# A sort by permutation matmuls, moved in part to indirect DMA writes, and a gather ring of 16 rows

## Chip, cores, metric

The kernel runs on one core of one Trainium2 chip. The metric is the device time of one execution in microseconds. Engines are named as in the profile: PE (TensorE), DVE (VectorE), ACT (ScalarE), POOL (GpSimd), SP (SyncE). POOL can issue DMAs whose row addresses stand in SBUF (indirect DMAs).

## The reference, cut to what matters

Four layers on x of 1250 x 1024 with 21250 edges (src, dst, type 0 to 7, weight), sorted by dst. Only the first two speak of edges:

```python
h  = sigmoid(layernorm(x) @ wenc.T + benc)            # 1250 x 500
h2 = h @ conv_weight
agg = segment_sum(h2[src] * edge_weight[:, None], dst)
x = x + ((agg + h @ lin_weight.T) @ wdec.T + bdec)    # layer 0, graph part
# dense mixture of 4 experts; then layer 1, graph part:
for r in range(8):                                    # relations
    out += (segment_sum(x[src] * (type == r), dst) / max(count[r], 1)) @ weight[r]
# gate, then 8 routed experts
```

## The kernel before

**Slots.** Rows are padded to 1280, ten tiles of 128. The edges come in as a 128 x 167 table (ET = 167 columns; partition p holds edges 167p to 167p + 166). They are regrouped into 176 slots (SLOTS) of 128 lanes, so that all edges of a slot go to one tile of destination rows. DVE computes for each edge its place, a lane and a slot (`sort`, lines 1213 to 1242, and lines 1281 to 1285), and packs source, relation and row into one number (`e_pack`, lines 1286 to 1288).

**The list.** To move each edge to its place, PE multiplies: for each of the 167 columns DVE builds a 128 x 128 matrix of lanes (`perm_lane`, line 1296) and a 128 x 352 matrix that holds pack and weight in the column of the slot (`perm_val`, lines 1297 and 1298), in a ring of four, and PE accumulates `perm_lane.T @ perm_val` in one PSUM bank (`permute`, line 622). PE has 120 of these put between other matmuls by `next_column` (line 629): one behind each matmul of the encoder from its third group on (80, line 643) and behind each of the h2 product (40, line 661). The other 47 run in a loop of PE behind them (lines 668 to 674). Then follow on PE the ten tiles of `h @ lin` (`from_h(A_LIN, KE)`, line 677, its matmuls also line 661), which ACT copies into `agg`. Meanwhile DVE unpacks the list out of PSUM (lines 1312 to 1322) and signals `list_ready`.

**Slot sums of layer 0.** For each slot POOL gathers 128 rows of h2 (2 KB each) from DRAM by an indirect DMA (`gather_slots`, line 521) into a ring of 8 rows (RING) in the region `room`. It runs in a loop: a copy of eight indices into `at_ring` (line 512) once in eight slots, and a wait for PE once in four (BATCH). ACT makes the weighted one-hot matrix of the slot, from one that DVE made for four slots at once (lines 1339 and 1340). PE multiplies both with the gathered rows (`slot_sum`, line 680: matmuls of lines 685 and 686) into one of four PSUM banks. DVE loads the slot's tile number into a register (line 1346) and adds the bank to that tile of `agg` (line 1351), each add behind the one before. PE may be four slots ahead of DVE, POOL eight ahead of PE. The wait of POOL for the first ring row that is used again lies behind PE's lin products, as slot sums do.

**Afterwards.** The decoder reads `agg` by transposes; then come the experts of layer 0, the relation products and root and gate products of layer 1 (PE, in split precision), in whose time POOL gathers 176 x 128 inverse counts of 4 bytes (line 540), then the slot sums of layer 1 (line 521 again, rows of 4 KB, PE lines 820 and 821, DVE line 1535), the gate, and the routed experts. The kernel ends with ten unrolled indirect gathers of POOL (line 575), each followed by an add of DVE (line 1701) and a store.

**Queues.** SP issues the plain loads in program order: edges, x, weights, constants; then waits for the encoder to load the decoder weights and the decoder bias, and for the slot sums before the experts' weights.

Of the kernel before, what the change touches and what calls it, by code (L numbers as in the profile page):

```python
# [30 lines left out]
P = 128  # L31
# [13 lines left out]
RING = 8  # L45
BATCH = 4
SLOTS = -(-((N_EDGES + NT * (P - 1)) // P) // RING) * RING
# [4 lines left out]
E1 = 8  # L52
# [4 lines left out]
NOWHERE = 1.0e6  # L57
# [5 lines left out]

UNIT_ENC, UNIT_CONVLIN, UNIT_DEC = 0, 1, 2
# [42 lines left out]
def build(nc, a, out):  # L107
    ctx = ExitStack()
    with ctx:
# [16 lines left out]
        moe_dram = dram("moe_rows", (TSLOTS * P, D))  # L126

# [18 lines left out]
        rows_h2 = room[:].rearrange("p b (c n) -> p (b c) n", n=EMBP)  # L146
# [46 lines left out]
        e_slot = scratch(ET)  # L193
        e_pack = e_key
# [112 lines left out]
        (rows_in,) = sems(RING, "rows_in")  # L307
# [55 lines left out]
        def _(sp):  # L363
# [39 lines left out]
            sp.wait_ge(slot_summed, RING + SLOTS)  # L403
# [42 lines left out]
            sp.wait_ge(slot_summed, RING + 2 * SLOTS)  # L446
# [40 lines left out]
        def _(pool):  # L487
# [17 lines left out]

            def gather_slots(table, at_list, rows, done, rounds_done):

                with pool.Fori(0, SLOTS // (2 * RING)) as i:
                    for half in range(2):


                        pool.tensor_copy(at_ring[:, half, :], at_list[:, bass.ds(2 * RING * i + half * RING, RING)]).then_inc(at_ready, 1)  # L512
                        for k in range(RING):
                            if k % BATCH == 0:

                                pool.wait_ge(slot_summed, done + 2 * RING * i + half * RING + k + BATCH)
# [11 lines left out]
            gather_slots(h2_dram, l_src, lambda k: rows_h2[:, k, :], 0, 0)  # L528
# [4 lines left out]
            pool.wait_ge(rows_in[RING - 1], 16 * SLOTS // RING)  # L533
            inv_rows = inv_dram.rearrange("n (r o) -> (n r) o", o=1)
            with pool.Fori(0, SLOTS // RING) as i:
                pool.tensor_copy(at_ring[:, 0, :], l_inv_at[:, bass.ds(RING * i, RING)]).then_inc(at_ready, 1)
                pool.wait_ge(at_ready, SLOTS // RING + i + 1)
# [15 lines left out]
            gather_slots(y_dram.rearrange("n r d -> (n r) d"), l_row8, lambda k: rows_y[:, k, :], SLOTS, 2 * SLOTS // RING)  # L553
# [4 lines left out]
            rounds = 3 * SLOTS // RING  # L558
# [22 lines left out]
        def _(pe):  # L581

            mm = nc.tensor.matmul
            pe.sem_inc(slot_summed, RING)
# [95 lines left out]
            def slot_sum(i, k, first=False):  # L680
                if not first or k >= 4:
                    pe.wait_ge(slot_added, RING * i + (k - 3))
                pe.wait_ge(hot_ready, RING * i + k + 1)
                pe.wait_ge(rows_in[k], 16 * i + 16)
                mm(sum_bank[k % 4][:, EMBC:EMBP], hot1[:, k, :], hotr[:, k, :], start=True, stop=True)
                mm(sum_bank[k % 4][:, 0:EMBC], hot[:, k, :], rows_h2[:, k, 0:EMBC], start=True, stop=True).then_inc(slot_summed, 1)  # L686
# [126 lines left out]
            def slot_sum2(i, k, first=False):  # L813
# [4 lines left out]
                pe.wait_ge(rows_in[k], 16 * i + 16 * (SLOTS // RING) + 16)  # L818
# [107 lines left out]
        def _(act):  # L926
# [34 lines left out]
            for m in range(NT):  # L961
                q = A_LIN + m
                act.wait_ge(a_full, q + 1)
                if m == 0:
                    act.wait_ge(perm_done, ET)
# [199 lines left out]
        def _(dve):  # L1165
# [47 lines left out]
            def sort(key, groups, cols, onehot, cum, pos, bank, full, tmp, between=lambda: None):  # L1213
# [25 lines left out]
                v.tensor_scalar(tmp, key, float(groups), NOWHERE, ALU.is_ge, ALU.mult)  # L1239
# [28 lines left out]
            link(v.tensor_copy(e_key, e_t0))  # L1268

# [8 lines left out]
            sort(e_key, NT, ET, e_hot, e_cum, e_pos, v_bank[0], V_PRE, e_lane, first_ln)  # L1278
# [10 lines left out]
            dve.wait_ge(room_zero, 1)  # L1289
# [12 lines left out]
            tail = (ET - head) % 4  # L1302
            for t in range(head):
                permute(t, t % 4, first=True)
            with dve.Fori(0, (ET - head - tail) // 4) as i:
                for j in range(4):
                    permute(4 * i + head + j, j)
            for t in range(ET - tail, ET):
# [33 lines left out]
            def add_slots(i, b, first=False):  # L1342

                for k in range(BATCH * b, BATCH * (b + 1)):
# [3 lines left out]
                    dve.wait_ge(slot_summed, RING * i + (RING + k + 1))  # L1348
# [182 lines left out]
            def add_slot2(i, k, first=False):  # L1531
                t = dve.value_load(l_tile[0:1, k:k + 1] if first else l_tile[0:1, bass.ds(RING * i + k, 1)], min_val=0, max_val=NT - 1)
                dve.wait_ge(slot_summed, RING * i + (SLOTS + RING + k + 1))
# [68 lines left out]
            sort(tok_key[:], E1, NT, tok_hot[:], tok_cum[:], tok_pos[:], v_bank[V_PRE2 % 2], V_PRE2, gsm[:, 0, :])  # L1602
# [131 lines left out]
```

## Time and profile before

| | us |
|---|---|
| median of three executions | 3163.37 |
| lowest, highest of them | 3155.08, 3163.69 |
| span of the profiled execution | 3157.0 |
| PE busy in it | 2859.9 (91%) |
| DVE, ACT, POOL busy in it | 1363.6, 592.5, 564.0 |
| mean clock granted to PE | 0.950 |

The span runs from the first instruction to the last of one more execution, taken by the profiler; its own time outside the span is not among the numbers shown, so the span is set beside the median. A matmul with float32 operands stands in the trace as two records. "Idle before" is the time that an engine stood still ahead of an instruction, with what ended it; "issue" means nothing that the profile shows. A clock of 1.00 is 2.4 GHz, 0.50 is 1.2 GHz.

### The profile page before, as it was taken

Reading aid. Unit: us, or ns where it says so; the run is one execution under the profiler, and the core shown is the slowest. Engines: PE = TensorE matmul, PEld = TensorE weight load, DVE = VectorE, ACT = ScalarE, POOL = GpSimd, SP = SyncE. Lnnn points to the kernel's source line nnn. Section 1 sums busy time; section 2 is a strip of 40 time slices with the busy share of each in tenths; the row PEclk is TensorE's granted clock in tenths of the full one; section 3 lists DMA queues with packets and bytes.
Section 4 is the critical chain, followed back from the end, with each engine's and each line's share of the span. In section 5 each row is a group of like instructions: output and inputs, shape, how many; then the busy total and the mean of one; then the engine's idle time right before and its main releaser. Section 6 shows DMA issues by size and latency. Waiting matters only on the chain.

```text
span 3157.0 us, 36610 instructions
## 1 busy us (share of the span) xinstructions
PE 2859.9 (91%) x11166; PEld 2026.2 (64%) x11166; DVE 1363.6 (43%) x2560; ACT 592.5 (19%) x1089; POOL 564.0 (18%) x673
## 2 busy tenths in 40 slices
PE   6999777879999997999999999999989998958884
PEld 3653222338888776888888888888854445836663
DVE  7664555454555464101001010112158887845453
ACT  2001121122333322212112121211010001123330
POOL 0002566100000002555400000000035551000001
PEclk9999888979999997999999999999999999979997
DMA  3012555203332323222212222311268883236664
GB/s 124 0 67 68 160 156 161 67 1 107 121 111 97 124 80 114 80 98 73 103 73 103 73 103 73 116 57 33 95 224 304 301 308 133 80 150 216 223 223 176
DMA packets 165619, 392.69 MB, mean 124 GB/s; under 512 B 22158, under 2 KB 22670, under 8 KB 165560
## 3 DMA queue, kind: packets, MB, share of 16 engines
q1 hardware_dynamic: 81208, 174.26, 15.8%
q0 software_dynamic: 49072, 153.09, 15.2%
q10 hardware_dynamic: 35280, 64.54, 5.5%
q8 instruction: 38, 0.62, 0.1%
q14 instruction: 21, 0.17, 0.0%
HBM read 316.94 MB, written 74.89 MB: 124 GB/s over the span
## 4 chain that ended last, share of the span: by engine, by line
PE 71%; DVE 7%; issue 4%; DMA 3%; DVEq 2%; ACT 2%; POOL 1%; ACTq 0%; SPq 0%; POOLq 0%; another core or an unknown queue 0%
PE pair L796 12%; PE pair L798 12%; PE pair L797 12%; PE pair L820 5%; PE pair L821 5%; PE pair L686 3%; PE pair L707 2%; PE pair L762 2%; PE pair L744 2%; PE pair L764 2%; PE pair L763 2%; PE pair L746 2%; PE pair L745 2%; DVE wl L1433 2%; DMA tok_raw<-in_L_ffn_w 2%
## 5 line engine op out<-in xcount | busy, mean ns | idle before, releaser
L796 PE MATMUL pair<-wh,xh 128*128 128x512 f32 x1600 | 623.4, 390 | 1.8 <-DVE xl L1185 1.8
L798 PE MATMUL pair<-wl,xh 128*128 128x512 f32 x1600 | 623.1, 389 | 0.0
L797 PE MATMUL pair<-wh,xl 128*128 128x512 f32 x1600 | 623.1, 389 | 0.0
L1433 DVE TENSOR_TENSOR wl<-raw,wh 128x512 fp32r<-128x512 f32 x352 | 221.5, 686 | 804.0 <-ACT wh L929 755.2
L796 PEld LDWEIGHTS pair<-wh,xh 128*128 128x128 f32 x1600 | 300.8, 188 | 64.6 <-issue 2.2
L797 PEld LDWEIGHTS pair<-wh,xl 128*128 128x128 f32 x1600 | 300.8, 188 | 62.7
L798 PEld LDWEIGHTS pair<-wl,xh 128*128 128x128 f32 x1600 | 300.7, 188 | 62.5
L929 ACT ACTIVATE wh<-raw 128x512 fp32r<-128x512 f32 x352 | 208.0, 627 | 334.8 <-PE pair L764 164.0
L929 ACT ACTIVATE OS<-pair 128x512 f32<-128x512 f32 x170 | 101.3, 596 | 742.7 <-PE pair L798 618.6
L1535 DVE TENSOR_TENSOR X<-pair,X 128x1024 f32 x176 | 215.5, 1225 | 52.5 <-PE pair L821 37.8
L686 PE MATMUL pair<-room,XN 128*128 128x504 f32 x352 | 215.2, 728 | 0.0
L1351 DVE TENSOR_TENSOR U<-pair,U 128x512 f32 x176 | 121.7, 691 | 167.1 <-PE pair L686 63.3
L521 POOL DMA_INDIRECT room<-h_rows,at_ring x176 | 169.1, 961 | 133.9 <-PE pair L686 69.2
L820 PE MATMUL pair<-W,XN 128*128 128x512 f32 x352 | 181.3, 597 | 9.4 <-DMA W<-y_rows,at_ring 9.1
L521 POOL DMA_INDIRECT W<-y_rows,at_ring x176 | 165.4, 940 | 136.1 <-PE pair L821 92.6
L540 POOL DMA_INDIRECT inv_ring<-inv_count,at_ring x176 | 169.2, 961 | 67.9 <-issue 50.4
L821 PE MATMUL pair<-W,XN 128*128 128x512 f32 x352 | 180.6, 595 | 0.0
L744 PE MATMUL pair<-xh,wh 128*128 128x384 f32 (+1 forms) x384 | 138.5, 361 | 10.1 <-DVE wl L1433 10.1
L512 POOL COPY at_ring<-l_row 128x8 int32 x22 | 4.4, 200 | 760.9 <-PE pair L798 760.8
L762 PE MATMUL pair<-wh,hh 128*128 128x512 f32 x320 | 126.6, 396 | 12.9 <-DVE hl L1469 11.2
L745 PE MATMUL pair<-xl,wh 128*128 128x384 f32 (+1 forms) x384 | 137.5, 358 | 0.0
L746 PE MATMUL pair<-xh,wl 128*128 128x384 f32 (+1 forms) x384 | 137.4, 358 | 0.0
(249 smaller groups left out, 3732.7 us busy)
## 6 DMA issues: line engine op xcount, KB each, us to landing
y_rows<-OS ACTq DMA_DIRECT2D x160, 256.0 KB
raw<-in_L_gnn_weight SPq DMA_DIRECT2D x16, 2048.0 KB
raw<-in_L_ffn_w SPq DMA_DIRECT2D x12, 2048.0 KB
raw<-in_L_ffn_w SPq DMA_DIRECT2D x24, 1024.0 KB
tok_raw<-in_L_ffn_w SPq DMA_DIRECT2D x7, 2048.0 KB
tok_raw<-in_L_ffn_w SPq DMA_DIRECT2D x14, 1024.0 KB
U<-in_L_ffn_b SPq DMA_DIRECT2D x18, 512.0 KB
moe_rows<-OS ACTq DMA_DIRECT2D x36, 256.0 KB
```

What stands on the lines that cost most here:

```text
L521: pool.indirect_dma_start(rows(k), None, table, bass.IndirectOffsetOnAxis(ap=at_ring[:, half, k:k + 1], axis=0)).then_inc(rows_in[k], 16)
L686: mm(sum_bank[k % 4][:, 0:EMBC], hot[:, k, :], rows_h2[:, k, 0:EMBC], start=True, stop=True).then_inc(slot_summed, 1)
L744: mm(o, wh[:, k, part], xh[:, k, cols], start=(k == 0), stop=False)
L745: mm(o, wh[:, k, part], xl[:, k, cols], start=False, stop=False)
L796: mm(o, xh[:, k, cols], wh[:, k, :], start=(k == 0), stop=False)
L797: mm(o, xl[:, k, cols], wh[:, k, :], start=False, stop=False)
L798: last = mm(o, xh[:, k, cols], wl[:, k, :], start=False, stop=(k == KD - 1))
L820: mm(pair[:, 0:HALF], hot[:, k, :], rows_y[:, k, 0:HALF], start=True, stop=True)
L821: mm(pair[:, HALF:D], hot[:, k, :], rows_y[:, k, HALF:D], start=True, stop=True).then_inc(slot_summed, 1)
L929: return nc.scalar.activation(dst, src, func, **kw)
L1433: v.tensor_tensor(wl[:, k, :], raw[:, k, :], wh[:, k, :].bitcast(F32), ALU.subtract).then_inc(wl_ready, 1)
L1535: v.tensor_tensor(u_rows[:, bass.ds(t, 1), :], pairs[(k + 1) % 4][:].rearrange("p (o n) -> p o n", o=1), u_rows[:, bass.ds(t, 1), :], ALU. ...
```

## The change

120 of the 167 columns (SCATTERED) are no longer permuted. The place of an edge is turned into the number of a row of 8 bytes (pack and weight) in a DRAM table `list_dram`, lane times 176 plus slot. SP fills the table with zeros early, DVE makes indices and records (`e_at`, `e_rec`, in the second half of XN), and POOL writes each of the 120 columns with an indirect DMA, 128 records at a time. When all have landed SP loads the table back (`l_part`), and DVE adds it to what PE has accumulated of the other 47 columns. Padding edges get places beyond the part that is read (NOWHERE). PE's 47 permutes all stand between encoder matmuls; the loop behind h2 is gone.

The gathers of layer 0 are unrolled, take their indices from the list itself, and use a ring of 16 rows (RING0) in the region XT, which is free then. All counts that start with the ring's size are shifted. One wait of POOL ahead of the inverse counts, for the last gathered row, is gone.

```diff
+RING0 = 16
+SCATTERED = 120
-NOWHERE = 1.0e6
+NOWHERE = float((1 << 20) + P - 1)
+PERMUTED = ET - SCATTERED
+        list_rows = (P - 1) * SLOTS + (int(NOWHERE) >> 7) + ET
+        list_dram = dram("list_rows", (list_rows + 1, 2))
-        rows_h2 = room[:].rearrange("p b (c n) -> p (b c) n", n=EMBP)
+        rows_h2 = XT[:].rearrange("p k n -> p (k n)")[:, 0:RING0 * EMBP].rearrange("p (b n) -> p b n", n=EMBP)
+        e_rec = XN[:, 1, 0:2 * ET].rearrange("p (t c) -> p t c", c=2)
+        e_at = XN[:, 1, 2 * ET:3 * ET].bitcast(I32)
+        l_part = XN[:, 1, 3 * ET:3 * ET + 2 * SLOTS].rearrange("p (s c) -> p s c", c=2)
...
+            sp.wait_ge(room_zero, 1)
+            sp.dma_start(list_dram[0:P * SLOTS, :].rearrange("(p s) c -> p (s c)", s=SLOTS), room[:, 0, 0:2 * SLOTS]).then_inc(list_zero, 16)
+            sp.wait_ge(scattered, 16 * SCATTERED)
+            sp.dma_start(l_part, list_dram[0:P * SLOTS, :].rearrange("(p s) c -> p s c", s=SLOTS)).then_inc(list_in, 16)
             sp.wait_ge(a_full, A_H2)
             dec = W[:, UNIT_DEC % 2, :].rearrange("p (k n) -> p k n", k=KE)
             sp.dma_start(dec, wide(a["decT"])).then_inc(w_in[UNIT_DEC % 2], 16)
...
-            sp.wait_ge(slot_summed, RING + SLOTS)
+            sp.wait_ge(slot_summed, RING0 + SLOTS)
...
+            pool.wait_ge(list_zero, 16)
+            pool.wait_ge(scatter_ready, 1)
+            for t in range(ET - SCATTERED, ET):
+                pool.indirect_dma_start(list_dram, bass.IndirectOffsetOnAxis(ap=e_at[:, t:t + 1], axis=0),
+                                        e_rec[:, t, :], None).then_inc(scattered, 16)
...
-            gather_slots(h2_dram, l_src, lambda k: rows_h2[:, k, :], 0, 0)
+            for s in range(SLOTS):
+                if s >= RING0 and s % BATCH == 0:
+                    pool.wait_ge(slot_summed, s + BATCH)
+                pool.indirect_dma_start(rows_h2[:, s % RING0, :], None, h2_dram,
+                                        bass.IndirectOffsetOnAxis(ap=l_src[:, s:s + 1], axis=0)
+                                        ).then_inc(rows_in[s % RING0], 16)
...
-            pool.wait_ge(rows_in[RING - 1], 16 * SLOTS // RING)
...
-            pe.sem_inc(slot_summed, RING)
+            pe.sem_inc(slot_summed, RING0)
...
-            column = iter(range(ET))
+            column = iter(range(PERMUTED))
...
             def next_column():
-                t = next(column)
-                permute(t, t % 4, first=(t == 0))
+                t = next(column, None)
+                if t is not None:
+                    permute(t, t % 4, first=(t == 0), final=(t == PERMUTED - 1))
...
             from_h(A_H2, 0, next_column)
-            begun = next(column)
-            tail = (ET - begun) % 4 or 4
-            with pe.Fori(0, (ET - begun - tail) // 4) as i:
-                for j in range(4):
-                    permute(4 * i + begun + j, (begun + j) % 4)
-            for t in range(ET - tail, ET):
-                permute(t, t % 4, final=(t == ET - 1))
...
-            for k in range(RING):
+            for k in range(RING0):
                 slot_sum(0, k, first=True)
-            with pe.Fori(1, SLOTS // RING) as i:
-                for k in range(RING):
+            with pe.Fori(1, SLOTS // RING0) as i:
+                for k in range(RING0):
                     slot_sum(i, k)
...
-                v.tensor_scalar(tmp, key, float(groups), NOWHERE, ALU.is_ge, ALU.mult)
+                v.scalar_tensor_tensor(tmp, key, float(groups), far, ALU.is_ge, ALU.mult)
...
+            v.tensor_scalar(e_slot, iota_free[:, 0:ET], float(P), NOWHERE, ALU.mult, ALU.add)
...
-            dve.wait_ge(room_zero, 1)
+            dve.wait_ge(t_full, T_LN1 + 2 * NT)
+            v.tensor_copy(e_rec[:, :, 0], e_pack)
+            v.tensor_copy(e_rec[:, :, 1], e_w)
+            link(v.scalar_tensor_tensor(e_at, e_lane, float(SLOTS), e_slot, ALU.mult, ALU.add))
+            v.sem_inc(scatter_ready, 1)
+            dve.wait_ge(list_zero, 16)
...
-            dve.wait_ge(perm_done, ET)
-            v.tensor_copy(l_w[:], list_bank[:, SLOTS:2 * SLOTS])
-            link(v.tensor_copy(l_pack[:], list_bank[:, 0:SLOTS]))
+            dve.wait_ge(perm_done, PERMUTED)
+            dve.wait_ge(list_in, 16)
+            v.tensor_tensor(l_w[:], list_bank[:, SLOTS:2 * SLOTS], l_part[:, :, 1], ALU.add)
+            link(v.tensor_tensor(l_pack[:], list_bank[:, 0:SLOTS], l_part[:, :, 0], ALU.add))
```

## Rows read from the trace of the kernel before

**Rows 1.** The page: the chain that ended last, by engine
```profile
PE 71%; DVE 7%; issue 4%; DMA 3%; DVEq 2%; ACT 2%; POOL 1%; ACTq 0%; SPq 0%; POOLq 0%; another core or an unknown queue 0%
```

**Rows 2.** Windows, by stage: us, busy us (instructions) of PE, PEld, DVE, ACT, POOL; clock; DMA
```profile
57.35:217.67 160.32, 160.30 (x480) 90.81 (x479) 103.84 (x369) 12.07 (x20) 0.00 (x0) 1.00 0.08 28
217.67:252.88 35.21, 35.21 (x98) 14.81 (x96) 33.86 (x134) 0.60 (x1) 0.00 (x0) 1.00 0.07 23
...
288.35:577.97 289.62, 217.79 (x529) 73.81 (x529) 150.91 (x260) 55.65 (x175) 166.94 (x188) 0.85 0.55 152
```

**Rows 3.** Timeline, interleaved stretch: start, us, engine, line, tiles [idle before]
```profile
208.11 1.02 PE L661 MATMUL pair<-W,U 128*128 128x512 f32 x2
...
209.56 1.02 PE L661 MATMUL pair<-W,U 128*128 128x512 f32 x2
```

**Rows 4.** Timeline, from the last permute to the first gather
```profile
252.88 34.50 PE L661 MATMUL pair<-W,U 128*128 128x512 f32 x80
...
256.08 0.34 DVE L1322 SCALAR_TENSOR_TENSOR l_inv_at<-l_tmp,l_rel 128x176 int32<-128x176 f32 x1
...
258.34 1.17 POOL L521 DMA_INDIRECT room<-h_rows,at_ring  x1 [0.92 <-POOL at_ring L512]
```

**Rows 5.** Timeline, the ninth gather; source L521, who waited for it
```profile
293.30 0.97 POOL L521 DMA_INDIRECT room<-h_rows,at_ring  x1 [24.83 <-PE pair L686]
...
  PEld pair L685: 22.0, 12
  PE pair L685: 13.7, 22
```

**Rows 6.** Timeline, DVE ahead of the permutes
```profile
56.33 0.33 DVE L1286 SCALAR_TENSOR_TENSOR U<-U 128x167 f32<-128x167 int32 x1
...
57.35 0.29 DVE L1296 TENSOR_SCALAR room<-iota_free,U 128x128 f32<-128x128 f32 x1
```

**Rows 7.** Timeline of POOL, end of a round of count gathers
```profile
1241.80 0.94 POOL L540 DMA_INDIRECT inv_ring<-inv_count,at_ring  x1 [0.30 <-issue]
1244.78 0.19 POOL L545 COPY l_inv<-inv_ring 128x8 f32 x1 [2.04 <-DMA inv_ring<-inv_count,at_ring]
```

**Rows 8.** Timeline, first and last of the ten unrolled gathers at the end
```profile
3126.13 0.94 POOL L575 DMA_INDIRECT XT<-moe_rows,tok_posi  x1 [53.91 <-DMA moe_rows<-OS]
...
3140.23 1.81 POOL L575 DMA_INDIRECT XT<-moe_rows,tok_posi  x1 [0.30 <-issue]
```

**Rows 9.** DMA issues of the whole span: xcount, KB, us to landing
```profile
W<-in_decT SPq DMA_DIRECT2D x1, 2048.0 KB, 7.7
...
b_dec<-in_L_gnn_bdec SPq DMA_DIRECT2D x1, 512.0 KB, 3.6
...
inv_count<-count ACTq DMA_DIRECT2D x1, 40.0 KB, 7.5
```

**Rows 10.** Timeline, a held add and PE's wait for it
```profile
355.37 0.69 DVE L1351 TENSOR_TENSOR U<-pair,U 128x512 f32 x1 [3.55 <-remote]
...
356.30 0.17 PE L685 MATMUL pair<-hotr,hot 128*128 128x8 bf16 x1 [3.12 <-DVE U L1351]
```

**Rows 11.** Waits, slot stage of layer 0: us, times, longest
```profile
POOL room L521 <- PE pair L686: 69.2, 17, 24.8
```

**Rows 12.** Windows of L1351 (adds), then L521 (gathers): us, busy (x), clock, DMA
```profile
399.00:412.00 13.00, 8.09 (x12) 0.75 0.47 126
424.00:438.00 14.00, 4.15 (x6) 0.76 0.62 180
508.00:524.00 16.00, 4.45 (x7) 0.93 0.69 192
...
399.00:412.00 13.00, 7.43 (x8) 0.75 0.47 126
424.00:438.00 14.00, 8.10 (x8) 0.76 0.62 180
508.00:524.00 16.00, 9.85 (x12) 0.93 0.69 192
```

More of the change, by code:

```diff
@@ L306, in build @@
         (os_out,) = sems(4, "os_out")
-        (rows_in,) = sems(RING, "rows_in")
+        (rows_in,) = sems(RING0, "rows_in")
+        list_zero, scatter_ready, scattered, list_in = map(sem, ("list_zero", "scatter_ready", "scattered", "list_in"))
         (moe_in,) = sems(NT, "moe_in")
@@ L444, in _ @@
                 sp.dma_start(raw1[j][:], wide(top[1][4 * j * P:4 * (j + 1) * P, :])).then_inc(raw1_in, 16)
-            sp.wait_ge(slot_summed, RING + 2 * SLOTS)
+            sp.wait_ge(slot_summed, RING0 + 2 * SLOTS)
             for k in range(4):
@@ L514, in gather_slots @@
                             if k % BATCH == 0:
-                                pool.wait_ge(slot_summed, done + 2 * RING * i + half * RING + k + BATCH)
+                                pool.wait_ge(slot_summed, done + 2 * RING * i + half * RING + k + BATCH + RING0 - RING)
                                 pool.sem_inc(issued, 1)
@@ L667, in _ @@
             from_h(A_H2, 0, next_column)
-            begun = next(column)
-            tail = (ET - begun) % 4 or 4
-            with pe.Fori(0, (ET - begun - tail) // 4) as i:
-                for j in range(4):
-                    permute(4 * i + begun + j, (begun + j) % 4)
-            for t in range(ET - tail, ET):
-                permute(t, t % 4, final=(t == ET - 1))
+            assert next(column, None) is None
             from_h(A_LIN, KE)
@@ L681, in slot_sum @@
                 if not first or k >= 4:
-                    pe.wait_ge(slot_added, RING * i + (k - 3))
-                pe.wait_ge(hot_ready, RING * i + k + 1)
+                    pe.wait_ge(slot_added, RING0 * i + (k - 3))
+                pe.wait_ge(hot_ready, RING0 * i + k + 1)
                 pe.wait_ge(rows_in[k], 16 * i + 16)
-                mm(sum_bank[k % 4][:, EMBC:EMBP], hot1[:, k, :], hotr[:, k, :], start=True, stop=True)
-                mm(sum_bank[k % 4][:, 0:EMBC], hot[:, k, :], rows_h2[:, k, 0:EMBC], start=True, stop=True).then_inc(slot_summed, 1)
-            for k in range(RING):
+                mm(sum_bank[k % 4][:, EMBC:EMBP], hot1[:, k % RING, :], hotr[:, k % RING, :], start=True, stop=True)
+                mm(sum_bank[k % 4][:, 0:EMBC], hot[:, k % RING, :], rows_h2[:, k, 0:EMBC], start=True, stop=True).then_inc(slot_summed, 1)
+            for k in range(RING0):
                 slot_sum(0, k, first=True)
-            with pe.Fori(1, SLOTS // RING) as i:
-                for k in range(RING):
+            with pe.Fori(1, SLOTS // RING0) as i:
+                for k in range(RING0):
                     slot_sum(i, k)
@@ L964, in _ @@
                 if m == 0:
-                    act.wait_ge(perm_done, ET)
+                    act.wait_ge(perm_done, PERMUTED)
                 copy(agg[:, m, :], a_bank[q % 2][:]).then_inc(a_read, 1)
@@ L1211, in keep_scores, with sort @@
                     v.tensor_copy(rows[0:n, lo:lo + cnt], v_bank[(q + g) % 2][0:n, 0:cnt]).then_inc(v_read, 1)
-            def sort(key, groups, cols, onehot, cum, pos, bank, full, tmp, between=lambda: None):
+            def sort(key, groups, cols, onehot, cum, pos, bank, full, tmp, far, between=lambda: None):
                 gs = slice(0, groups)
@@ L1276, in first_ln @@
                 normalise(1, T_LN1)
-            sort(e_key, NT, ET, e_hot, e_cum, e_pos, v_bank[0], V_PRE, e_lane, first_ln)
+            sort(e_key, NT, ET, e_hot, e_cum, e_pos, v_bank[0], V_PRE, e_lane, e_slot, first_ln)
             slot_groups(l_tile[:], l_tmp[:], SLOTS, NT)
@@ L1301, in _ @@
             head = 4
-            tail = (ET - head) % 4
+            tail = (PERMUTED - head) % 4
             for t in range(head):
                 permute(t, t % 4, first=True)
-            with dve.Fori(0, (ET - head - tail) // 4) as i:
+            with dve.Fori(0, (PERMUTED - head - tail) // 4) as i:
                 for j in range(4):
                     permute(4 * i + head + j, j)
-            for t in range(ET - tail, ET):
+            for t in range(PERMUTED - tail, PERMUTED):
                 permute(t, t % 4)
-            dve.wait_ge(perm_done, ET)
-            v.tensor_copy(l_w[:], list_bank[:, SLOTS:2 * SLOTS])
-            link(v.tensor_copy(l_pack[:], list_bank[:, 0:SLOTS]))
+            dve.wait_ge(perm_done, PERMUTED)
+            dve.wait_ge(list_in, 16)
+            v.tensor_tensor(l_w[:], list_bank[:, SLOTS:2 * SLOTS], l_part[:, :, 1], ALU.add)
+            link(v.tensor_tensor(l_pack[:], list_bank[:, 0:SLOTS], l_part[:, :, 0], ALU.add))
             link(v.tensor_scalar(l_row8[:], l_pack[:], (1 << ROWSHIFT) - 1, None, ALU.bitwise_and))
@@ L1601, in _ @@
             link(v.tensor_tensor(tok_key[:], top_f[:, :, 0], tok_pad[:], ALU.add))
-            sort(tok_key[:], E1, NT, tok_hot[:], tok_cum[:], tok_pos[:], v_bank[V_PRE2 % 2], V_PRE2, gsm[:, 0, :])
+            v.tensor_scalar(gsm[:, 1, :], iota_free[:, 0:NT], 0.0, NOWHERE, ALU.mult, ALU.add)
+            sort(tok_key[:], E1, NT, tok_hot[:], tok_cum[:], tok_pos[:], v_bank[V_PRE2 % 2], V_PRE2, gsm[:, 0, :], gsm[:, 1, :])
             slot_groups(slot_exp[:], slot_tmp[:], TSLOTS, E1)
```

12 lines of the change are left out of this document (6 added, 6 removed).

## The prediction

> **What bounds the kernel now.** I read the page's chain first [rows 1]: PE holds 71% of it, so a microsecond taken from work beside PE is worth nothing unless PE waits there, or does work that the change removes. The table by stage [rows 2] shows such places. After 577.97 us nothing that the change touches costs time. Before it lie four stretches: the encoder and h2 matmuls with 120 permutes between them (57.35 to 217.67, PE full), the 47 permutes left over (217.67 to 252.88, PE full), the lin matmuls (to 288.35), and the slot sums (to 577.97), where PE is busy 217.79 of 289.62 us, its granted clock is 0.85, and no engine is full.
>
> In the first stretch [rows 3] one 128x512 matmul, a permute and the next matmul take 1.45 us (208.11 to 209.56). The 40 lin matmuls of that size (two records each) take 34.50 us, 0.86 each [rows 4], so a permute between matmuls costs PE 0.59 us. The 47 left over go at 35.21/47 = 0.75 us, the pace of the three DVE instructions that make their operands. Then comes the hand-over [rows 4]: the last permute ends at 252.88, DVE has unpacked the list at 256.42, the first gather goes at 258.34. Eight gathers lie ready early; the ninth waits for a ring row until 293.30, because PE does lin first [rows 5].
>
> **Part 1, the sort.** PE loses 73 interleaved permutes, 73 x 0.59 = 43 us, and the stretch of the 47, 35 us. It would be through with lin at 288 - 43 - 35 + 1 = 211 us. But the list now needs 120 DMA writes first, and they set its time:
> - DVE starts permuting at 57.35, and the write indices are made just before that: two copies and one scalar_tensor_tensor on 128x167, which go at 0.34 us each there (three from 56.33 to 57.35 [rows 6]), and two small additions in and before the sort, 0.3 together: 1.3 us. Ready at 58.6; POOL wakes 0.3 us after a DVE signal, as I count from 256.42: 58.9. The indices' wait for the layer norm's transposes costs nothing, PE being in the encoder by 57.35 [rows 2].
> - POOL issues an indirect DMA each 1.25 us (0.94 busy, 0.30 between), for 4-byte pieces as for rows of 2 KB [rows 5, 7]. No row prices a write by index. From below: 1.25 us, for the same 128 descriptors. From above: the unrolled gathers at the end, nine steps in 3140.23 - 3126.13 = 14.1 us, 1.57 each [rows 8], which run beside VectorE adds. I take 1.25, as nearest in kind are the small pieces. With 0.2 for a slower first one and 119 x 1.25 the last goes at 207.9 and lands 2.98 us later (1241.80 to 1244.78 [rows 7]), 210.9.
> - The DMA engines' own part: the count store is 1280 pieces of 32 B, 80 for each of 16 engines, and lands in 7.5 us [rows 9], at most 0.09 us a piece. A column has 8 per engine, 0.75 us, under the 1.25 of the issue, so POOL hides it; the price if it does not is a rival below.
> - SP fetches the 180 KB back. A load of 512 KB landed in 3.6 us [rows 9]; I take 2.8 and 0.3 to wake: 214.0. The decoder weights, queued on SP behind that wait, leave some 48 us later. They are used at 580, so being late costs nothing, but their 2 MB take 7.7 us [rows 9] and meet the first gathers: 2 us.
> - DVE's unpacking stays 3.4 us, POOL wakes in 0.3: first gather at 217.7 instead of 258.34. PE idles from 211, so the list, not PE, sets the start.
>
> The first row lands about 3.1 us on, so slot sums start at 220.8 instead of 288.35: 67.5 us earlier. Against that stand 2 us because PE begins after ten idle microseconds, at the low clock (stretches with a restart show 0.75 [rows 12]), and the 2 us of the decoder weights.
>
> **Part 2, the ring of 16 and the unrolling.** They remove POOL's waits for PE in this stage, 69.2 us in 17 waits, of which the first, 24.8, is already counted above [rows 11], and POOL's copy and second wait once in eight. What this could reach is POOL's own pace, 176 x 1.25 = 220 us in place of 289.6, a gain of 69. But PE waited for gathered rows only 22.0 + 13.7 = 35.7 us [rows 5]. What holds the stage is DVE's add: that of 355.37 came after 3.55 idle us, with the sum long there, and PE then stood 3.12 us for it, four banks being all it has [rows 10]. Between two adds DVE only loads the tile number into a register (line 1346). In stretches the adds come slow or quick [rows 12]: in 399 to 412 there are 12, one per 1.08 us, with 8 gathers; in 424 to 438 and 508 to 524 there are 13 in 30 us with 20 gathers, while POOL goes on without a stop.
> - So POOL's lead falls by 4/13 = 0.31 a us in the quick stretch and grows by 7/30 = 0.23 in the slow ones. Where the two balance, 43% of the time is quick and a slot takes 1/(0.43 x 12/13 + 0.57 x 13/30) = 1.55 us, near the measured 289.6/176 = 1.65. The ring's size is not in this sum: it makes the swings longer and leaves their mix. I take no gain and no loss. The loss side: quick stretches half as common, 1/(0.215 x 0.92 + 0.785 x 0.43) = 1.86 us a slot, +38 us. The gain side: -69.
> - The rest ends at nothing: the second slot stage only gets shifted counts, and the wait of POOL that goes ahead of the inverse counts lies far before PE's first relation product, for which POOL waits anyway. The later layers move as they are.
>
> **Sum.** -67.5 + 2 + 2 = -63.5 us against the profiled execution: 3157.0 - 63.5 = 3093.5 of span. The median shown, 3163.37, is 6.4 above that span, so I forecast 3100 us. A measurement of this kernel can tell 0.3%, 9.5 us, from nothing.
>
> **The rivals.**
> - *The ring pays (0.18).* If DVE's held loads come with POOL's stops and restarts, or if the deeper lead keeps PE at full clock, the stage goes at the 1.25 us of the issue: 3100 - 69 = 3031. For it: the clock is 0.75 and 0.76 in two of the three stretches [rows 12], and slots at low clock are slower than POOL. Against it: the slow adds lie within POOL's long runs, and a deeper ring makes these longer.
> - *The writes go slower beside VectorE, or the slow stretches grow (0.17).* At the 1.57 us of the unrolled gathers [rows 8] the list is 120 x 0.32 = 38 us later: 3138, with PE idle 48 us ahead of the slot sums. The loss side of part 2 gives 3138 too. For it: DVE is busy 103.84 of 160.32 us beside the interleaved permutes [rows 2], here until the 47 are done, at 126. Against it: that covers 54 of the 120 writes. The Trainium skill, "SBUF — State Buffer", section "Who interferes with whom", says that copy and tensor_scalar can enter a mode that holds the port pair shared with GpSimd for a whole instruction. By that rule each of the 54 could be held for one instruction of DVE of some 0.3 us [rows 6], 16 us in all: 3116.
> - *Slower: the small writes themselves take the time (0.08).* The place is the DMA engines from 59 us to the list. If a column's writes had to be finished before the next one's began, a column would cost the 2.98 us of a landing [rows 7] in place of 1.25: 120 x 1.73 = 208 us later, 3308. It decides from 1.25 + 63.5/120 = 1.78 us a column; above that the list comes too late for any gain. Against it: the count gathers come each 1.25 us without waiting for each other's landings, and the store of small pieces landed in 7.5 us [rows 7, 9]. The Trainium skill, "DMA: Bandwidth & Descriptors", section "Specifications", says that a transfer under 512 B does a read-modify-write; no row here has writes of 8 B.
> - *The forecast as worked out (0.57),* 3085 to 3115.
>
> **Range and chances.** Forecast and first two rivals hold 0.92. The range 3028 to 3145 takes them in and leaves out the slow tail. Faster by over 0.3% (under 3154): 0.57 + 0.18 + most of 0.17, which can come with other small losses: 0.87. Within 0.3%: 0.05. Slower: 0.08.
>
> **What would show it.** Right: 120 DMA issues of POOL from about 59 us at 1.25; 47 permutes, all before 127; PE through with lin near 211 and idle to 221; slot sums over 280 to 295 us, with adds still in quick and slow stretches; all after them moved by one amount. Wrong: a pitch of the writes over 1.3 us, or their last landing over 5 us; a slot stage under 270 or over 305 us, or adds that are held differently; a first gather far behind the last write, which would put a cost on SP's queue.

## The result, and the profile after

The changed kernel took 3203.43 us (median of four, 3196.76 to 3210.92) against 3160.04 for the kernel before on the same chip: ratio 1.0143, interval 1.0122 to 1.0164. It is 43 us slower where 60 faster was forecast. The profiled execution took 3201.72 us at a span of 3199.9. Later runs show that this sign goes with the chip: on another chip the same kernel is 2.8% faster. So each time below stands against the kernel before on the same chip.

First GpSimd's writes and SP's fetch of the list, by tile (first and last start):

```profile
L522 POOL DMA_INDIRECT list_rows<-XN x120: 954/958/1271, 58.9 to 212.2; - x120
L406 SPq DMA_DIRECT2D XN<-list_rows x1: 320/320/320, 214.3 to 214.3; - x1
```

These are the steps of the forecast, the last write 4 us after its 207.9. But the table of windows, with the columns of [rows 2], over the time of the writes and over the slot sums reads:

```profile
57.00:218.00 161.00, 62.20 (x108) 24.98 (x106) 24.95 (x82) 2.06 (x3) 115.35 (x120) 0.63 0.02 2
...
343.00:623.60 280.60, 209.75 (x529) 78.82 (x529) 150.29 (x260) 55.78 (x176) 157.10 (x160) 0.82 0.54 150
```

PE is busy 62 of 161 us where it was full [rows 2], and the clock falls to 0.63. The timeline of DVE shows a column each 11.2 us in place of 1.45 ("remote" names a releaser that the profile can't place), until three columns start 0.8 us apart once POOL has been silent for 15 us:

```profile
156.82 0.29 DVE L1320 TENSOR_SCALAR room<-iota_free,U 128x128 f32<-128x128 f32 x1 [10.32 <-remote]
...
200.93 0.29 DVE L1320 TENSOR_SCALAR room<-iota_free,U 128x128 f32<-128x128 f32 x1 [10.30 <-remote]
212.12 0.35 DVE L1320 TENSOR_SCALAR room<-iota_free,U 128x128 f32<-128x128 f32 x1 [10.13 <-remote]
221.94 0.29 DVE L1320 TENSOR_SCALAR room<-iota_free,U 128x128 f32<-128x128 f32 x1 [8.71 <-remote]
227.57 0.28 DVE L1320 TENSOR_SCALAR room<-iota_free,U 128x128 f32<-128x128 f32 x1 [4.79 <-remote]
228.39 0.28 DVE L1320 TENSOR_SCALAR room<-iota_free,U 128x128 f32<-128x128 f32 x1
229.16 0.28 DVE L1320 TENSOR_SCALAR room<-iota_free,U 128x128 f32<-128x128 f32 x1
```

PE, in its timeline, takes each column about 1 us after DVE began it:

```profile
157.85 1.54 PE L645 MATMUL pair<-room 128*128 128x352 f32 x2 [8.04 <-DVE room L1322]
```

DVE may not make a column before PE has read the one four back. An engine learns that another is done by a counter that the other raises; I call that a signal. The column of 200.93 needed the signal of the one that DVE began at 156.82 and PE multiplied at 157.85 to about 159.4. So DVE learned some 42 us late of a matmul that had ended. The other direction is prompt. ScalarE learns late too. Here are its next two evictions after that of 69.42, and ahead of the second the matmul of PE that it needed, the last of its group of eight:

```profile
140.58 0.69 ACT L969 ACTIVATE U<-pair,b_enc 128x512 f32<-128x512 f32 x1 [70.47 <-remote]
180.76 1.83 PE L667 MATMUL pair<-XT,W 128*128 128x512 f32 x2
227.41 0.69 ACT L969 ACTIVATE U<-pair,b_enc 128x512 f32<-128x512 f32 x1 [86.14 <-remote]
```

About half of the 86.14 us is PE's own slow group, which needs eight columns. But that matmul had ended at 182.6, so 45 us of the wait are the signal's. It was sent between those of the permutes at 179.43 and 190.68, and it came at 227.41, between the columns of 221.94 and 227.57 that these two released. PE's signals thus arrive in the order in which they were sent, though they go to two engines.

The rest follows. The encoder and h2 are late, and the first row gather waits for the last store of h2 (timeline of POOL):

```profile
212.21 0.96 POOL L522 DMA_INDIRECT list_rows<-XN  x1 [0.30 <-issue]
312.42 1.00 POOL L550 DMA_INDIRECT XT<-h_rows,l_src  x1 [99.25 <-DMA h_rows<-OS]
```

Slot sums run from 343.1 to 623.6 in place of 288.35 to 577.97 [rows 2]: they begin 55 us later and take 9 us less. After them the kernel is the same.

### The profile page after: what moved, and what is told of

The parts are those of the page before. It is cut to its first block, busy times and chain, and to the rows that moved or that the text cites. A ratio compares the mean times of both kernels' runs of the same rounds, so it can differ in the third digit from the quotient of the medians.

```text
span 3199.9 us, 35021 instructions
## 1 busy us (share of the span) xinstructions
PE 2796.1 (87%) x10926; PEld 1991.2 (62%) x10926; DVE 1267.8 (40%) x2205; ACT 591.9 (18%) x1089; POOL 674.1 (21%) x771
## 4 chain that ended last, share of the span: by engine, by line
PE 74%; DVE 9%; another core or an unknown queue 4%; issue 4%; DMA 3%; DVEq 3%; ACT 2%; POOL 0%; ACTq 0%; SPq 0%; POOLq 0%
PE pair L814 11%; PE pair L816 11%; PE pair L815 11%; PE pair L838 5%; PE pair L839 5%; PE pair L704 3%; PE pair L725 2%; PE pair L685 2%; PE pair L762 2%; PE pair L764 2%; PE pair L763 2%; PE pair L780 2%; PE pair L782 2%; PE pair L781 2%
## 5 line engine op out<-in xcount | busy, mean ns | idle before, releaser
L550 POOL DMA_INDIRECT XT<-h_rows,l_src x176 | 172.3, 979 | 224.1 <-DMA h_rows<-OS 99.2
L704 PE MATMUL pair<-XT,XN 128*128 128x504 f32 x352 | 208.7, 733 | 0.0
L645 PE MATMUL pair<-room 128*128 128x352 f32 x94 | 46.2, 579 | 106.0 <-issue 73.2
```

The source lines that it names most:

```text
L550: pool.indirect_dma_start(rows_h2[:, s % RING0, :], None, h2_dram, bass.IndirectOffsetOnAxis(ap=l_src[:, s:s + 1], axis=0)).then_inc(rows_ ...
L704: mm(sum_bank[k % 4][:, 0:EMBC], hot[:, k % RING, :], rows_h2[:, k, 0:EMBC], start=True, stop=True).then_inc(slot_summed, 1)
```

## The experiments

The runs fell on two kinds of chip. On some, the one of the first result among them, the kernel before took 3153 to 3160 us; I call these the **late** chips. On two others it took 3114 and 3117 us, the **prompt** chips. One late chip was met twice and was late both times; no other is known to have been, so whether this is the chip itself or a state that lasts is not shown. The expectations stand as written before each run; those of the first four kernels (e1 to e4) know nothing yet of two kinds.

**Ring and unrolling alone** (late: 3154.23 against 3155.82; prompt: 3080.61 against 3114.19).

```diff
-SCATTERED = 120
+SCATTERED = 0
...
```

The rest of the edit takes out the writes and the fetch of the list and puts PE's loop of 47 permutes back.

> Only the ring of 16 and the unrolled gathers; no edge column is written by GpSimd, all 167 are permuted. Theory (a long unbroken stream of indirect DMAs from GpSimd makes the other engines learn of TensorE's signals tens of microseconds late): the sort is as in the kernel before, permutes at 1.45 us a column, lin done near 288 us, because GpSimd is silent there; the slot sums have the gathers beside them as before and take 280 to 290 us; time 3150 to 3165. Rival (the unrolled gathers or the ring of 16 are what costs the 43 us): 3200. Rival from the prediction (the ring pays): slot sums near 220 us, time 3090.

> Ring of 16 and unrolled gathers alone, once more, for a chip on which the signals are late (kernel before 3158 us). There the slot sums should take about 280 us as in the changed kernel, in place of 290 us (rows ready ahead: 16 in place of 8), begin near 288 us and the time be 3145 to 3158. If it were the ring or the unrolling that costs, 3200. On a chip that takes 3114 us for the kernel before: 3081 us again.

Ratios 0.9892 (0.9876 to 0.9909) on a prompt chip and 0.9989 (0.9973 to 1.0005) on a late one. So these parts don't cost the 43 us. And the same instructions give two slot stages: 288.7 to about 503 us on the prompt chip, 288.6 to 580 on the late one. The adds of DVE show why; here by tile, what they waited for and who waited for them, first prompt, then late:

```profile
L1367 DVE TENSOR_TENSOR U<-pair,U x176: 682/691/693, 290.0 to 502.7; 128x512 f32 x176
...
  PE pair L701: 77.8, 88
  DVE U L1367: 14.5, 48
  issue: 1.4, 9
...
  PEld pair L700: 9.2, 14
```

```profile
  issue: 88.0, 58
  PE pair L701: 46.1, 19
...
  remote: 13.8, 3
...
  PE pair L700: 53.7, 26
```

On the late chip the adds stand 102 us for "issue" and "remote", and PE's matmuls stand 53.7 us for adds; on the prompt one the adds stand 1.4 us so, and only weight loads stand for them, 9.2 us. That is the held add of [rows 10].

**DVE's permutes written out**, waits and addresses constant (prompt: 3028.89 against 3114.19; late: 3200.93 against 3158.05).

```diff
-            with dve.Fori(0, (PERMUTED - head - tail) // 4) as i:
-                for j in range(4):
-                    permute(4 * i + head + j, j)
-            for t in range(PERMUTED - tail, PERMUTED):
+            for t in range(head, PERMUTED):
```

> The changed kernel with VectorE's loop of permutes written out, so that its waits compare with constants and its addresses are constants. Theory (TensorE's signals arrive late, whatever form the wait has): no change, a column each 11.2 us beside the writes, a burst of columns at 227 us, time 3200. Rival (the loop's waits against a register, or its register addresses, are what goes slowly beside GpSimd's stream): permutes back at 1.45 us a column, list of the permuted part done by 130 us, lin done near 215 us, time 3100 to 3130.

> VectorE's permutes written out with constant waits, once more, beside the changed kernel on the same chip. Theory A (chip or state): within 0.3% of the changed kernel, whatever that takes here. Theory B (the loop's waits against a register were the cause): 3029 us, while the changed kernel takes 3150 us or more.

The first run looked like a win for the rival, 2.7% faster, and it was none: it had fallen on a prompt chip. Beside the unedited kernel on a late one it takes 1.0132 of the kernel before, with columns 11.2 us apart. Register waits are not the cause.

**The changed kernel unedited** (late: 3203.65 against 3158.05, 1.0149; prompt: 3030.12 against 3116.51, 0.9722, 0.9706 to 0.9738), and the kernel before.

> The changed kernel once more, unedited. The four runs before this one shared one chip, on which the kernel before took 3114 us and not 3160, and in none of them did VectorE's permutes wait for TensorE's signals beside the writes. Theory A (the late signals belong to a chip, or to a state of it, that not every chip shows): on a chip where the kernel before takes 3114 us, the changed kernel takes about 3029 us, permutes 1.45 us apart, and on one where it takes 3160 us, 3200 us. Theory B (the edits of the four kernels, unrolled waits or 8 buffers or pauses, cured it): 3150 us or above wherever it runs, columns 11.2 us apart beside the writes.

> The changed kernel unedited, in case this call falls on the chip where the kernel before takes 3114 us: there 3029 us is expected, as with its two variants. Elsewhere 3203 us again.

> The kernel before once more, unedited, for its trace on this chip. Theory A (late signals are a matter of the chip or its state): where it takes 3114 us in place of 3160, the 46 us are missing in the stretch 290 to 580 us, where slot sums and adds run beside GpSimd's gathers: VectorE's adds no longer held 3.5 us for TensorE's signal, slot sums near 240 us in place of 290. Rival: the 46 us lie spread over the whole kernel, as a faster clock or memory would give.

The kernel before met a late chip again (3155.07), so its trace on a prompt one is missing. The windows of the changed kernel on the prompt chip, beside those above:

```profile
57.00:218.00 161.00, 152.75 (x416) 78.50 (x414) 43.91 (x148) 18.64 (x31) 115.68 (x120) 0.99 0.08 21
...
226.00:451.00 225.00, 194.81 (x528) 59.94 (x528) 149.14 (x259) 53.64 (x168) 166.19 (x173) 0.99 0.72 203
```

POOL's busy time beside the encoder is the same, 115.7 and 115.4 us, and PE's is 152.8 in place of 62.2. The timeline of PE has the hand-over as forecast: lin done at 210.8, then the wait for the first row.

```profile
204.65 6.17 PE L685 MATMUL pair<-W,U 128*128 128x512 f32 x14
225.95 0.17 PE L703 MATMUL pair<-hotr,hot 128*128 128x8 bf16 x1 [15.13 <-DMA XT<-h_rows,l_src]
```

From the end of the slot sums the two chips need the same: 3199.9 - 623.6 = 2576.3 us and 3027.4 - 451 = 2576.4. The whole difference lies ahead of that. Layer 1's slot sums too, with their 176 indirect gathers, take the same on both: POOL issues these gathers from 2359.2 to 2663.0 and from 2185.7 to 2490.8. It does so mostly in fours, with 41 waits for PE of 2.2 us on average between them on either chip.

**Eight operand buffers in place of four** (prompt: 3030.68 against 3114.19; late: 3202.97 against 3155.82).

```diff
...
-                    dve.wait_ge(perm_done, t - 3)
+                    dve.wait_ge(perm_done, t - 7)
...
```

> The changed kernel with 8 buffers of 512 floats for the permutes' operands in place of 4 buffers of 1024. If each signal is late by a fixed 43 to 45 us, eight columns are under way in that time: a column each 5.6 us, some 26 columns by 212 us instead of 17, and most of the rest of the sort hidden sooner; ScalarE's evictions still wait as long. If instead signals are let through one at a time, the period stays 11.2 us and each is 90 us late. In both cases the span stays within 20 us of the changed kernel's, as ScalarE waits for TensorE's signals for its evictions too: 3180 to 3205.

> The changed kernel with 8 operand buffers for the permutes, once more, for a chip on which the signals are late (kernel before 3158 us). If each signal is late by a fixed 43 to 45 us: a column each 5.6 us beside the writes. If they are let through one at a time, 11.2 us apart: a column each 11.2 us still. Time 3185 to 3205 in both. On a chip that takes 3114 us for the kernel before: 3030 us again.

On the late chip the period stayed 11.2 us. The column that DVE began at 205.97 needed the one eight back, which PE multiplied at 117.28 (timelines of DVE and PE):

```profile
205.97 0.49 DVE L1321 TENSOR_SCALAR room<-iota_free,U 128x128 f32<-128x128 f32 x1 [10.35 <-remote]
```

```profile
117.28 1.54 PE L646 MATMUL pair<-room 128*128 128x352 f32 x2 [3.52 <-issue]
```

That signal was 87 us late, twice as late with twice as many under way. So it is no fixed delay. By itself this would also fit a VectorE that gets through one wait in 11.2 us, since four and eight such periods are 45 and 90 us. ScalarE, whose buffers were not touched, rules that out. Its eviction of 223.35 needed the matmul that ended at 136.2, so it too was 87 us late, where it was 45 us late with four operand buffers:

```profile
133.04 1.01 PE L668 MATMUL pair<-XT,W 128*128 128x512 f32 x1 [3.02 <-issue]
135.15 1.01 PE L668 MATMUL pair<-XT,W 128*128 128x512 f32 x1 [1.10 <-issue]
...
223.35 0.69 ACT L970 ACTIVATE U<-pair,b_enc 128x512 f32<-128x512 f32 x1 [88.22 <-remote]
```

So TensorE's signals stand in one queue, whoever they are for, and come through at a set pace, one column in 11.2 us, about the time of nine issues of POOL; more buffers only lengthen the queue. With eight under way PE itself stands some 3 us ahead of each encoder matmul, for nothing that the profile shows.

**120 extra indirect reads in the kernel before** (late: 3291.30 against 3158.05, ratio 1.0424, 1.0396 to 1.0452).

```diff
...
+            pool.wait_ge(perm_ready, 1)
+            for t in range(120):
+                pool.indirect_dma_start(extra[:, 2 * t:2 * t + 2], None, extra_dram,
+                                        bass.IndirectOffsetOnAxis(ap=extra_at[:], axis=0)).then_inc(extra_in, 16)
```

> The kernel before with 120 extra indirect reads of 8 bytes a partition, back to back on GpSimd beside the encoder, from the first permute on; nothing waits for them but GpSimd. Late signals, where the chip shows them, come from the unbroken stream of indirect DMAs and not from writes to DRAM: then permutes go to a column each 5 us or slower for 150 us and the time rises by over 40 us above the kernel before. Rival (only writes do it, or this chip doesn't show it): the permutes stay at 1.45 us a column and the time is within 0.3% of the kernel before.

No write to DRAM, no list, no ring of 16, and yet the same picture. By tile, and from DVE's timeline:

```profile
L512 POOL DMA_INDIRECT extra<-in_gate_wT,extra_at x120: 940/944/1196, 59.1 to 212.0; - x120
```

```profile
98.05 0.29 DVE L1306 TENSOR_SCALAR room<-iota_free,U 128x128 f32<-128x128 f32 x1 [9.65 <-remote]
...
109.25 0.29 DVE L1306 TENSOR_SCALAR room<-iota_free,U 128x128 f32<-128x128 f32 x1 [10.35 <-remote]
```

On a late chip the cause is POOL's unbroken stream of indirect DMAs, of either direction. It cost 133 us here.

**Bursts of 4 with a wait for their landing, 120 columns** (prompt: 3065.34 against 3114.19, 0.9839; late: 3136.63 against 3155.82, 0.9938, 0.9915 to 0.9961).

```diff
+                n = t - (ET - SCATTERED)
+                if n and n % 4 == 0:
+                    pool.wait_ge(scattered, 16 * n)
```

> The changed kernel, but GpSimd waits for the landing of every 4 writes before it issues the next 4. Theory (only an unbroken stream holds TensorE's signals back; a pause of 2 us lets them through): permutes at 1.45 us a column and encoder as in the kernel before, the 47 permutes done near 130 us, the 120 writes take 120 x 1.26 + 29 x 2 to 3 us = 210 to 240 us and end at 270 to 300 us, after lin; the list comes at about 275 to 305 and first slot sum at 280 to 310: time 3140 to 3170. Rival (each indirect DMA holds the signals back, paused or not): columns still 5 us apart or more and time 3200 or above.

> The changed kernel with GpSimd waiting for the landing of every 4 writes, once more; the first time the chip was one without late signals (kernel before 3114 us). Where the kernel before takes 3158 us and the changed one 3203: if a pause of about 1.6 us after each 4 writes is enough for TensorE's signals to come through, the permutes stay 1.45 us apart, the writes end at 250 us, slot sums begin near 262 us and, at the 280 us that they took in the changed kernel, end at 542 in place of 624: 3120 us. If pauses of that length don't help: columns 5 us or more apart and 3180 us or more. On a chip that takes 3114 us for the kernel before: 3065 us again.

On the late chip the permutes and the encoder are back at full pace. The first window, which was 36.31 us of PE in the unbroken stream, reads:

```profile
57.00:130.00 73.00, 72.55 (x205) 38.67 (x204) 42.47 (x145) 4.81 (x7) 44.67 (x46) 1.00 0.02 1
```

A break of 1.6 us after each 4 issues (45.5 us in 29 waits) cures that stretch and costs 37 us at its end: the last write goes at 249.6. The time came 17 us over my figure, as slot sums began at 262.2, as expected, but took about 290 us.

**96 columns in bursts of 4** (late: 3099.46 against 3155.82, 0.9811, 0.9788 to 0.9834). The edit is the one above, with SCATTERED = 96.

> 96 columns written in bursts of 4 with a wait for their landing, 71 permuted, in place of 120 and 47. From the bursts of 4 seen before (120 writes from 59 to 250 us, 1.6 us each): the writes end at 59 + 96 x 1.6 = 213 us, the first slot sum can begin near 225; TensorE has 24 columns more at 0.65 us, so lin is done near 211 + 16 = 227 us. Slot sums begin near 230 us, 32 us earlier than with 120 in bursts: where the kernel before takes 3114 us, 3033 us; where it takes 3158 us, 3088 us, if pauses let the signals through.

List and lin are ready together: slot sums from 226.4. They take 298 us in place of the 280 assumed, and the time is 11 us over mine. It is 56 us faster than the kernel before on a late chip; it did not run on a prompt one.

**The same in bursts of 8** (prompt: 3021.84 against 3116.51, 0.9695; late: 3148.50 against 3152.96, 0.9983, 0.9960 to 1.0006).

> 96 columns written in bursts of 8 in place of 4, the gathers unpaced. In the changed kernel the first columns beside the unbroken stream still came 1.45 us apart until about 70 us, that is for the first 8 or 9 writes. If a burst of 8 is short enough: writes 1.41 us each, end at 59 + 96 x 1.45 = 198 us, the permutes stay 1.45 us apart; lin, not the list, then sets the start of the slot sums (227 us): 3099 us, no gain over bursts of 4. If 8 in a row already hold signals back: some columns of each burst 3 us or more apart, the encoder later, 3110 us or more.

> 96 columns in bursts of 8, once more. On the chip without late signals it took 3022 us. On a chip with them: if a burst of 8 is short enough, the permutes stay 1.45 us apart beside the writes and the time is 3090 to 3100 us, as with bursts of 4; if not, gaps of 3 us and more open between columns, the encoder is late by tens of us and the time 3110 us or more.

On the late chip a burst of 8 with a break of 1.4 us is too long. In the window 130 to 215 us PE is busy 55.71 us, where bursts of 4 give 84.39, and slot sums begin at 289.9. On the prompt chip this is the fastest kernel of the study.

**Row gathers paced too** (by 8: prompt 3095.38 against 3116.51, 0.9933; late 3094.65 against 3152.96, 0.9809, 0.9788 to 0.9830. By 4, with `s % 4` in the first line: prompt 3165.69, 1.0161). The edit comes on top of 96 columns in bursts of 4.

```diff
+                if s and s % 8 == 0:
+                    pool.wait_ge(rows_in[(s - 1) % RING0], 16 * ((s - 1) // RING0 + 1))
```

> 96 columns in bursts of 4, and besides the layer-0 row gathers paced: before each eighth gather GpSimd waits for the landing of the one before. On a chip with late signals (kernel before 3158 us) the slot sums took 298 us with 96 columns, of which GpSimd's issue is 176 x 1.25 = 220 us. If the late signals are what stretches the slot stage and 8 in a row are short enough, a gather costs 1.25 + 2.3 / 8 = 1.54 us, the stage takes 271 us and the time falls from 3099 to 3072 us. Rival (the stage is held by something else, or 8 in a row already delay the signals): 298 us or more, 3099 us or more. On a chip without them (3114 us for the kernel before) the pauses only cost.

> The same with the pause before each fourth gather. Pauses then cost 2.3 / 4 a gather: 1.83 us, the stage 176 x 1.83 = 321 us, 3122 us, whatever the signals do; VectorE's adds should never wait more than 1 us for a signal of TensorE whose matmul has ended. If even so adds are held for 3 us and more, the stage is not held by GpSimd's stream.

> 96 columns in bursts of 4, row gathers paced by 8, once more. On the chip without late signals it took 3095 us, some 60 us more than unpaced variants there, so a pause costs about 2.7 us: 22 of them. On a chip with late signals (3158 us for the kernel before): if these stretch the slot stage (298 us unpaced) and 8 in a row are short enough, the stage takes the same time as it did on the other chip and the kernel about 3095 us there too, with no add of VectorE held 3 us for an ended matmul; the gain over 3099 us would be nil, since pauses cost what the held signals do. If 8 in a row already delay the signals, or something else holds the stage: 3120 us or more.

Paced, the kernel takes the same time on both kinds of chip, 3095 us, and the slot stage nearly so (matmuls from 226.3 to 515.4 and to 516.8). So with pauses the difference between chips is gone here too. On the late chip they save 8 us of the 298; on the prompt one the same stage takes 213.5 us unpaced (226.3 to 439.8, the kernel with bursts of 8) and 289 paced. My price for a pause, 2.3 us, was too low; with a pause at every fourth gather the stage takes 358 us, not 321. Both rows of adds, prompt then late, by tile:

```profile
  PE pair L709: 126.2, 112
  DVE U L1381: 11.7, 39
  issue: 0.2, 1
```

```profile
  PE pair L709: 71.9, 57
  issue: 43.8, 39
```

On the late chip 43.8 us of held adds remain, now in the shadow of the pauses. A wait after 8 gathers thus does not remove the delay. This kernel beats the one before on both kinds, by 1.9% and 0.7%, as the 120 columns in bursts of 4 do by 0.6% and 1.6%. None was found that is best on both.

## Why the prediction failed

**The step that failed** is "PE loses 73 interleaved permutes ... It would be through with lin at 211 us", with its listed sign, 47 permutes all before 127. I priced the writes on POOL, on the DMA engines and on SP, and took every handshake (one engine's wait for another's signal) beside them as it stood in a trace where POOL was silent there. On a late chip TensorE's signals come one column in 11.2 us beside the stream, and lin was done at 342.2, 131 us after the forecast. The 120 reads in the kernel before show this cause alone. The measured span, 3199.9, is 106 us over the forecast 3093.5. Slot sums start 122 us later than forecast; they give back 9, the work behind them 3, and 4 stood in the sum already for two small losses.

**The sign that stood in the rows.** The held add [rows 10] came after 3.55 idle us, released by "remote". Its sum was older still. PE may be four slots ahead, so the matmul at 356.30, which waited for this add, lies four behind the one whose sum it took (timeline of the kernel before):

```profile
347.00 1.09 PE L686 MATMUL pair<-room,XN 128*128 128x504 f32 x2
```

That had ended 7 us before the add. I wrote that between two adds DVE only loads the tile number, and so made it a matter of DVE. The same adds on a prompt chip stand 1.4 us in all. With the sort, where reads and writes alike cause it, that points to the same late signal, in the stage of the kernel before that has POOL's stream beside a handshake; by itself this cause was not isolated in the slot stage, as pauses of 8 left part of the holds. The change put such a stream, longer and unbroken, beside a tighter handshake.

**What held.** First write 58.9 (58.87), last 207.9 (212.2, at 1.26 us with one stumble), fetch at 214.3 where I had it landed at 214.0. The rival of small writes at 2.98 us each is refuted by that pitch, and DVE's operations did not lengthen the issues: those of the writes are 958 ns in the median while DVE makes columns on the prompt chip as well. So the 16 us that the Trainium skill's "SBUF — State Buffer", section "Who interferes with whom", would have given don't appear, where 46 of DVE's columns lie beside writes; whether these instructions were in that mode no run shows.

**Part 2, "no gain and no loss".** On late chips the number is right (0.9989; the stage took 9 us less within the changed kernel) and the reason is not: the held adds, which I took for a matter of DVE, are missing on a prompt chip. There ring and unrolling gain 33.6 us, about half of the 69 of the rival "the ring pays", and the stage goes at the pace of POOL's issue, as that rival said.

**On a prompt chip the forecast's path is there.** Lin is done at 210.8 (211 forecast), slot sums begin at 225.95 (220.8; 4.7 of the 5 us are the later last write, 212.6). The gain is 86.4 us, of which 33.6 come with ring and unrolling. The 52.8 left are 14.7 short of the 67.5 of part 1: the stage begins 62.7 us earlier (226.0 against 288.7 with the ring alone), and takes 225 us where it takes 214 with the ring alone. Both stages go at POOL's pace. With the ring alone 16 gathers lie ready when lin ends, and the other 160 leave from 293.0 to 495.5, 1.27 us apart; in the changed kernel all 176 leave beside the stage (by tile):

```profile
L550 POOL DMA_INDIRECT XT<-h_rows,l_src x176: 942/946/1492, 220.8 to 443.6; - x176
```

That makes the 11 us. The low clock at the restart costs nothing in the end: the first pair of matmuls needs 2.03 us, later ones 1.09, and by 243 us PE waits for rows again. A stage under 270 us stood among my signs of being wrong, and that is what it shows here: part 2's account does not hold on this chip. That 3030 us is nearly the 3031 of the rival is luck, as the kernel before takes 3117 us there and not 3163.

**The chances.** All three rivals priced a pace of POOL, of the DMA engines, of the ring or of the adds in the slot sums. None let the work beside the stream slow down, and 0.87 for faster was too sure for 120 new instructions put beside a stretch that had none. A rival "the held adds of the slot stage appear in the sort too" had a price in the rows: with 3.55 us of idling at each, 47 columns are some 47 x 3 = 140 us later, enough to turn the sign.

**What stays open.** What path TensorE's signals share with GpSimd's indirect DMAs; why only some chips show it, and whether one that does always will; whether signals of other engines are held as well. DVE's to PE were not (1.0 us from the start of a column's first instruction to PE's matmul).

## What to carry to other kernels

An engine's idle time ahead of an instruction whose producer has long ended, put down to "remote" or "issue" while GpSimd issues indirect DMAs back to back, was a late signal here, and moving more such DMAs beside a tight TensorE handshake multiplied it. Break the stream into fours with a wait for the landing (1.6 us) where TensorE's consumers need its signals each 1 or 2 us, and choose how many columns to move so that list and matmuls are ready together; deeper buffers don't help, since the signals queue. To tell a late signal from a slow consumer, look at a second engine that waits for the same producer: if both are late by the same time, and in the order of sending, it is the signals. And run a kernel and its rival on the same chip: here one edit looked 2.7% faster and was nothing, and the change itself is 2.8% faster on one chip and 1.4% slower on another.

## What the runs showed of the hardware that was not expected

- On late chips, beside an unbroken stream of indirect DMAs at 1.26 us, TensorE's signals for the permutes pass at one column in 11.2 us, reads and writes alike; 42 us late with four under way, 87 with eight. ScalarE gets the encoder's as late, 45 and 87 us, and in the order of sending.
- It begins after some nine issues (columns still 1.45 us apart until about 70 us, writes from 58.9), and ends 15 us after the last (212.2 to 227.4). The sort beside bursts of 4 with 1.6 us between is free of it, beside bursts of 8 with 1.4 us it is not.
- Chips of the same type differ by 1.3% in the kernel before and by 5.7% in the changed one (3203 and 3030 us), at the same time for all work after the slot sums.
- 120 indirect writes of 128 x 8 bytes go at the pace of GpSimd's issue, 1.26 us; where each four are waited for, they land in 2.1 us in the median (prompt chip).
- The gathers of layer 1, which waits of 2.2 us break into fours, go with slot sums that take the same on both kinds of chip.
